# A two-layer decoder on one core: new order of steps in the first layer's woven rounds

## What is computed

```python
x = x + kernel_attention(layernorm(x))        # A
x = x + cross_attention(layernorm(x), ctx)    # B, one head
h = layernorm(x, scale, shift)
x = x + causal_attention_16_heads(h)          # C, on the layernormed value of x
x = ... + moe(layernorm(.., scale, shift))    # D: router, 8 experts, top 2
```

## Time and profile before

| | us |
|---|---|
| median of 3 runs | 1689.74 (1689.53 to 1692.46) |
| profiled execution | 1689.45, its span 1687.8 |
| PE busy | 1285.4 (76%) |
| DVE busy | 998.3 (59%) |
| ACT busy | 522.3 (31%) |
| POOL busy | 415.1 (25%) |
| mean granted clock of PE | 0.857 |

### The profile page before, as it was taken

One profiled execution on the slowest core, in us unless ns is written; L12 is line 12 of the kernel. 1 busy time (PEld: TensorE's weight loads), 2 busy tenths in 40 slices (PEclk: granted clock), 3 DMA queues, 4 the chain that ended last, 5 costly groups with the idle time before them and its releaser, 6 DMA issues.

```text
span 1687.8 us, 24678 instructions
## 1 busy us (share of the span) xinstructions
PE 1285.4 (76%) x7936; PEld 890.2 (53%) x7936; DVE 998.3 (59%) x2156; ACT 522.3 (31%) x1279; POOL 415.1 (25%) x528
## 2 busy tenths in 40 slices
PE   2677868767877699981458977779787697986987
PEld 1554654644644366651237754467554475644755
DVE  4447557457455233325676765768656686677852
ACT  2214324324322222210125512346213363233620
POOL 1032143243253200006622111311212212032100
PEclk9778878878888799995679989779897799987988
DMA  9510010191014211101315310044100350104501
GB/s 376 217 28 1 19 28 13 34 408 49 25 46 198 59 47 44 44 29 45 117 39 98 86 40 12 10 101 111 40 12 2 86 122 21 32 11 88 114 5 46
DMA packets 69693, 122.37 MB, mean 73 GB/s; under 512 B 25404, under 2 KB 55100, under 8 KB 68032
## 3 DMA queue, kind: packets, MB, share of 16 engines
q1 hardware_dynamic: 63936, 110.04, 21.7%
q0 software_dynamic: 5632, 10.77, 2.3%
HBM read 67.69 MB, written 53.07 MB: 72 GB/s over the span
## 4 chain that ended last, share of the span: by engine, by line
PE 46%; issue 24%; DVE 12%; POOL 8%; DVEq 3%; ACT 3%; DMA 2%; POOLq 2%; SPq 0%; ACTq 0%
PE ps L1143 7%; PE ps L1390 5%; PE ps L1162 3%; PE ps L525 3%; PE ps L1316 3%; PE ps L1332 3%; PE ps L533 2%; POOL experts L1779 2%; PE ps L1302 2%; PE ps L1403 2%; PE ps L933 1%; PE ps L1041 1%; POOL headbd L681 1%; PE ps L504 1%; DVE probs L1999 1%
## 5 line engine op out<-in xcount | busy, mean ns | idle before, releaser
L1628 ACT ACTIVATE probs<-ps,small 100x361 f32<-100x361 f32 x256 | 141.3, 557 | 94.1 <-DVE small L2347 89.5
L2347 DVE TENSOR_REDUCE small<-ps 100x2 f32<-100x722 f32 x128 | 115.7, 906 | 36.2 <-PE ps L1302 36.2
L1143 PE MATMUL ps<-every,xT_t 128*128 x256 | 122.3, 601 | 0.4 <-issue 0.4
L1390 PE MATMUL ps<-hT,experts 128*128 128x400 f32 x288 | 117.1, 558 | 1.2 <-DVE small L730 1.2
L1316 PE MATMUL ps<-cst,probs 100*121 100x100 f32 x768 | 104.0, 271 | 8.1 <-DVE probsT L2355 7.7
L1316 PEld LDWEIGHTS ps<-cst,probs 100*121 100x121 f32 x768 | 94.8, 185 | 22.2 <-issue 13.7
L2355 DVE TENSOR_SCALAR probsT<-ps 121x600 f32<-121x600 f32 x128 | 99.2, 775 | 9.1 <-PE ps L1316 9.1
L1332 PE MATMUL ps<-probsT,values_ 121*32 121x100 f32 x1536 | 90.8, 253 | 0.9 <-DVE probsT L2355 0.9
L1302 PE MATMUL ps<-k_stack,q_stack 96*100 96x362 f32 x256 | 81.8, 400 | 6.3 <-ACT probs L1628 5.6
L473 POOL TENSOR_TENSOR small<-small,cst 100x2 f32<-100x2 f32 x56 | 11.1, 198 | 295.3 <-DVE small L453 295.2
L1390 PEld LDWEIGHTS ps<-hT,experts 128*128 128x128 f32 x288 | 59.6, 215 | 42.2 <-issue 14.1
(11 more groups left out here) (329 smaller groups left out, 2887.2 us busy)
## 6 DMA issues: line engine op xcount, KB each, us to landing
k_stack<-key_d SPq DMA_DIRECT2D x192, 90.5 KB, 3.1
tok_d<-wt SPq DMA_DIRECT2D x1, 14848.0 KB, 45.5
res_d<-wt SPq DMA_DIRECT2D x1, 14848.0 KB, 42.0
every<-e_d SPq DMA_DIRECT2D x8, 1536.0 KB, 11.6
ctxT<-ctxT_d SPq DMA_DIRECT2D x8, 726.0 KB, 4.3
key_d<-k_hi SPq DMA_DIRECT2D x32, 181.0 KB, 2.8
key_d<-k_lo SPq DMA_DIRECT2D x32, 181.0 KB, 3.4
gates<-gate_d SPq DMA_DIRECT2D x28, 200.0 KB, 4.4
```

Of the source, the lines that this page charges most:

```text
L1143: ins = e.matmul(ps[:, 2 * i + t % 2, :], xT_t[:, t % 2, c, :], every[:, bass.ds(base + (i * DC + c) * HID0, HID0)], start=(c == 0), stop= ...
L1390: ins = e.matmul(bank(2 * i + j % 2, n=NT), w[:, c, :], hT[:, c, :], start=(c == 0), stop=(c == DC - 1))
L1628: ins = e.activation(f_e[:, n % 2, i, 0:LC], bank(2 * (n % 2) + i, S, LC), ACT.Exp, bias=h_nm[:, n % 2, i:i + 1], accum_out=h_sum[:, b, h: ...
L2347: inc(e.tensor_reduce(h_nm[:, n % 2, 0:2], ps[0:S, 2 * (n % 2):2 * (n % 2) + 2, 0:LC], AX, ALU.max, negate=True), "F_nm")
```

## The change

- Each round takes its steps in the order behind, early half 0, behind, early half 1. 20 rounds instead of 18; all three passes are written out, no hardware loop.
- A's norm for the next group is done ahead, in early's steps 14 (statistics) and 16 (applied) on DVE, its root on POOL in 14; `norm_ahead` for group 0 stands before everything. `xin` is waited for there. A's turn on PE is now step 0, input product 1, and so on.
- The router later: its first half in behind's step 4, its second in attention step 0 (9), PE's products in that step behind the scores; PE waits for `r_placed` in attention step 3, POOL in step 7, and sends in steps 7, 9, 11 and 13 to 17. The reciprocal sums are spread on POOL in attention steps 12 and 18.
- Empty steps: in early at 4, 11 and 16 (on PE), in behind one or two ahead of the attention, and behind C's output and D's scores. Attention is 9 to 27 of 40.
- One sine for both halves (64x400), in early's step 4 of half 0, waiting for both angles.
- The quotients late: the exponentials of A and B are turned and multiplied undivided; each output is scaled by the reciprocal of its sum while it is added (two fused operations of 100x256 for each half). `A_p` and `B_p` go; `B_x` is new: PE waits for it before A's input product writes the same PSUM banks.

Order of PE's steps, before: round 13 `kq0 rT0 kq1 rT1`, 14 `Bs0 Co0 Bs1 Co1`, 15 `pT0 - pT1 -`, 16 `oT0 Dt0 oT1 Dt1`, 17 `out0 gate0 out1 gate1`. After: round 14 `rT0 kq0 rT1 kq1`, 15 `- Bs0 Co0 Bs1`, 16 `Co1 - - -`, 17 `- pT0 Dt0 pT1`, 18 `Dt1 oT0 gate0 oT1`, 19 `gate1 out0 - out1` (kq keys times query, rT the turned reciprocals, Bs scores of B, Co output product of C, pT and oT B's turn and context product, Dt D's turn, 0 and 1 the halves).

The diff, without the places where only empty steps are added:

```diff
@@ -98,7 +98,8 @@
...
 EXPERT_AT = (E1 - 1, *range(E1 - 1))
-ROUNDS, STEPS = 18, 19
+ROUNDS, STEPS = 20, 19
+SEND_AT = {7: 0, 9: 1, 11: 2, 13: 3, 14: 4, 15: 5, 16: 6, 17: 7}
@@ -147,7 +148,7 @@
...
     for _ in range(ROUNDS):
-        for st in (x0, y, x1, y):
+        for st in (y, x0, y, x1):
@@ -401,11 +402,11 @@
...
             names["A_" + n] = names.pop("A_" + sem_name)
-        for n in ("nm", "e", "p", "pTp", "pT", "oTp", "oT"):
+        for n in ("nm", "e", "pTp", "pT", "oTp", "oT"):
...
                 names[f"{stage_}_{n}"] = names.pop(f"{stage_}_AB{n}")
-        for n in ("kqTp", "kqT", "qbkp", "qbk", "s"):
+        for n in ("kqTp", "kqT", "qbkp", "qbk", "s", "x"):
@@ -923,10 +924,11 @@
...
                 p, q, t, bs = 2 * h, 2 * h + 1, tok(h), list(enumerate(seqs(h)))
-                yield
...
                 W(e, "A_hT", g, 1, h)
+                if g:
+                    W(e, "B_x", g - 1, 1, h)
@@ -959,7 +962,7 @@
...
                 yield
-                W(e, "A_p", g, 1, h)
+                W(e, "A_e", g, 1, h)
@@ -998,7 +1002,8 @@
...
                 yield
-                W(e, "B_p", g, 1, h)
+                yield
+                W(e, "B_e", g, 1, h)
@@ -1031,7 +1036,7 @@
...
-            def attend(g):
+            def attend(g, routed):
@@ -1071,24 +1076,24 @@
...
                         scores(n)
+                    if routed and n == 0:
+                        ahead(g - 1)
...
                         turn(n - 2)
+                    if routed and n == 3:
+                        e.wait_ge(r_placed.sem, r_placed.at(g - 1))
...
             def behind(g, routed):
-                yield
-                if routed:
-                    ahead(g - 1)
-                yield
+                for _ in range(3):
+                    yield
...
                     W(e, "C_hT", g, 1, h)
-                    if h == 1 and routed:
-                        e.wait_ge(r_placed.sem, r_placed.at(g - 1))
@@ -1096,10 +1101,12 @@
...
                 yield
-                yield from attend(g)
+                yield
+                yield from attend(g, routed)
...
                     yield
+                yield
@@ -1112,11 +1119,11 @@
...
                     yield
+                yield
...
             in_turn(early(0, 0), early(0, 1))
-            woven(early(1, 0), early(1, 1), behind(0, False))
-            with e.Fori(1, NG - 1) as g:
-                woven(early(g + 1, 0), early(g + 1, 1), behind(g, True))
+            for g in range(NG - 1):
+                woven(early(g + 1, 0), early(g + 1, 1), behind(g, g > 0))
@@ -1436,8 +1442,10 @@
...
                 yield
-                W(e, "A_ang", g, 1, h)
-                inc(e.activation(a_trig[:, t], a_ang[:, t], ACT.Sin), "A_trig")
+                yield
+                if h == 0:
+                    W(e, "A_ang", g, 1, 1)
+                    e.activation(a_trig, a_ang, ACT.Sin).then_inc(names["A_trig"].sem, 2)
@@ -1514,21 +1524,21 @@
...
                 yield
+                yield
...
                     yield
-                for _ in range(4):
+                for _ in range(5):
...
                     yield
-                yield
-                yield
+                for _ in range(3):
+                    yield
...
             in_turn(early(0, 0), early(0, 1))
-            woven(early(1, 0), early(1, 1), behind(0))
-            with e.Fori(1, NG - 1) as g:
+            for g in range(NG - 1):
@@ -1680,23 +1690,23 @@
...
             def early(g, h):
-                root_pool(e, "A_", g, h)
-                yield
-                if h == 0:
-                    e.wait_ge(ld["rows"].sem, 16)
-                W(e, "A_xn", g, 1, h)
-                inc(add_bias(x, xin, "A_out", h), "A_xb")
...
                 inc(e.tensor_tensor(a_rn[:, own(h)], a_ss[:, own(h)], cs("mhalf", S)[:, 0:HB], ALU.pow), "A_rn")
-                yield
-                for _ in range(7):
+                e.wait_ge(ld["rows"].sem, 16)
+                inc(add_bias(x, xin, "A_out", h), "A_xb")
+                yield
+                for _ in range(8):
...
                 yield
+                for _ in range(2):
+                    yield
+                if g + 1 < NG:
+                    root_pool(e, "A_", g + 1, h)
@@ -1720,16 +1730,21 @@
...
                 strips(0)
-                if routed:
-                    e.wait_ge(r_placed.sem, r_placed.at(g - 1))
+                yield
...
                         strips({1: 1, 7: 2, 11: 3}[n])
-                    if routed and n % 2 and n >= 3:
-                        send((n - 3) // 2)
+                    if n == 12:
+                        recips_pool(e, "C_", g, 0, 1)
+                    if n == 18:
+                        recips_pool(e, "C_", g, 1, 2)
+                    if routed and n == 7:
+                        e.wait_ge(r_placed.sem, r_placed.at(g - 1))
+                    if routed and n in SEND_AT:
+                        send(SEND_AT[n])
@@ -1740,25 +1755,23 @@
...
                     yield
-                yield
-                yield
+                for _ in range(3):
+                    yield
                 yield from attend(g, routed)
-                for h in range(2):
-                    recips_pool(e, "C_", g, h, h + 1)
-                    yield
-                yield
-                yield
+                for _ in range(4):
+                    yield
...
                     yield
-                for _ in range(4):
-                    yield
-
+                for _ in range(6):
+                    yield
+
+            for h in range(2):
+                root_pool(e, "A_", 0, h)
...
             e.wait_ge(ld["fill"].sem, 16)
-            woven(early(1, 0), early(1, 1), behind(0, False))
-            with e.Fori(1, NG - 1) as g:
-                woven(early(g + 1, 0), early(g + 1, 1), behind(g, True))
+            for g in range(NG - 1):
+                woven(early(g + 1, 0), early(g + 1, 1), behind(g, g > 0))
@@ -1885,12 +1898,15 @@
...
+            def norm_ahead(g, h):
+                e.wait_ge(ld["x"].sem, g * 16 + 16)
+                inc((yield from norm_dve(e, "A_", g, h, xin, xnX)), "A_xn")
+                yield
+
...
                 p, q, t, o = 2 * h, 2 * h + 1, tok(h), own(h)
-
-                if h == 0:
-                    e.wait_ge(ld["x"].sem, g * 16 + 16)
-                inc((yield from norm_dve(e, "A_", g, h, xin, xnX)), "A_xn")
+                norm = norm_ahead(g + 1, h) if g + 1 < NG else iter(())
+
@@ -1950,20 +1967,23 @@
...
                 yield
-                W(e, "A_e", g, 1, h)
-                e.reciprocal(a_rs[:, o], a_sum[:, o])
-                e.drain()
-                inc(e.tensor_tensor(lg, lg, a_rs[:, o].unsqueeze(2).broadcast_to([S, HB, S]), ALU.mult), "A_p")
...
                 W(e, "A_xb", g, 1, h)
-                add_out(x, p, h)
+                e.reciprocal(a_rs[:, o], a_sum[:, o])
+                e.drain()
+                for i, b in enumerate(seqs(h)):
+                    e.scalar_tensor_tensor(x[:, b, :], ps[0:S, p, i * D:(i + 1) * D], a_rs[:, b:b + 1], x[:, b, :],
+                                           ALU.mult, ALU.add)
+                e.drain()
                 inc((yield from norm_dve(e, "B_", g, h, x, xnX)), "B_xn")
+                yield
...
                 inc(e.tensor_scalar(b_qbk[:, o], bank(p, S, HB), 1.0, None, ALU.mult), "B_qbk")
+                next(norm, None)
@@ -1973,21 +1993,23 @@
...
                 yield
-                W(e, "B_e", g, 1, h)
-                e.reciprocal(b_rs[:, o], b_sum[:, o])
-                e.drain()
-                for b in seqs(h):
-                    ins = e.tensor_scalar(b_e[:, b, 0:LC], b_e[:, b, 0:LC], b_rs[:, b:b + 1], None, ALU.mult)
-                inc(ins, "B_p")
+                next(norm, None)
+                yield
...
                 W(e, "B_xb", g, 1, h)
-                e.tensor_tensor(xall[:, bass.ds(g * NB + HB * h, HB), :], tokens(q), x[:, o, :], ALU.add)
-                e.drain()
-                yield
-
-            def attend(g):
+                e.reciprocal(b_rs[:, o], b_sum[:, o])
+                e.drain()
+                for i, b in enumerate(seqs(h)):
+                    ins = e.scalar_tensor_tensor(xall[:, bass.ds(g * NB + b, 1), :].rearrange("p o n -> p (o n)"),
+                                                 ps[0:S, q, i * D:(i + 1) * D], b_rs[:, b:b + 1], x[:, b, :],
+                                                 ALU.mult, ALU.add)
+                inc(ins, "B_x")
+                e.drain()
+                yield
+
+            def attend(g, ways):
@@ -2014,32 +2036,33 @@
...
                         inc(e.reciprocal(h_rs[:, o, :], h_sum[:, o, :]), "C_rs")
+                    if n == 0:
+                        next(ways, None)
...
                 norms = [norm_dve(e, "C_", g, h, group, y) for h in range(2)]
-                next(norms[0])
-                next(ways, None)
-                yield
```

(20 more changed lines are left out.)

4 lines of the change are left out of this document (added).

## The result

The changed kernel takes 1680.7 us (median; 1680.4 to 1685.9) against 1689.7 for the kernel before: ratio 0.9947, 95% interval 0.9926 to 0.9967. A second comparison on another chip gave 0.9940 (0.9923 to 0.9957). So it is 9 to 10 us faster where 36 were forecast, and lies outside the range. The profiled execution after took 1685.9 (span 1684.2).

The account below looks back on a forecast made before the run. No engine is full: a pass is a chain of hand-overs between four in-order engines, mostly PE waiting for DVE. Passes -38.7, start +0.8, last group +1.8 give -36.1 us: 1653.4 us, range 1634 to 1674.

Parts of the forecast that it names:

- the three kinds of waits: PE's waits for A's divided probabilities and the quotient product gone, those for normed rows at B's turn near 0.
- mark to step 0: Pass start, norm ahead and router later: step 0 at 28.1 us instead of 33.2, -5.1; without router 25.2 instead of 31.1.
- Clock: PE's new idle stretches put ten microseconds of following work partly at half rate: +2.5 us a pass, bounds 0 and +6.
- Slower: Rival: DVE-paced rounds leave PE at the low level from step 5 to 18, +13 us a pass, 1728 us; 4%.
- Late quotients: In A, division leaves DVE's path between exponential and turn; PE's 10.7 us wait over six halves goes: -3.6 us a pass.
- the quotient product: B's late quotients and rear step first make it ready when PE asks; 12.0 us of waits go: -4.0 us a pass.
- The empty step: Behind A's output, one more round lets two attention steps in before B's turn, removing PE's waits: -3.6 us a pass.
- One sine: Steps 0 to 4: two table loads a pass fewer, both angles made before step 0; 15.8 us for four steps, -1.9.
- Start and last group: Kernel start +0.8 us (first combine product waits for the second sine), last group +1.8 us (router's second half in bare steps).
- Half of it: Rival: DVE takes the place, PE's removed waits return as waits for score evaluation; -19 us in all, 1670 us; 20%.
- sign of failure, a pass above 118 us: The prediction called itself wrong if a woven pass took above 118 us; it expected passes of 108 to 113.

Follow-up runs that it names:

- the filling: Changed kernel with 24 extra 100x400 bf16 matmuls on PE ahead of D's first turn in each of the four groups: ratio 0.9849, 1663 to 1671 us.
- the later norm: Changed kernel with the last half of the next group's first norm one round later on VectorE: ratio 0.9906.
- the front-first trace: Changed kernel with the order inside a round put back to front half 0, rear, front half 1, rear: ratio 0.9897, with all ten runs 0.9944.
- the late quotients alone: Kernel before with only the division of A's and B's weights dropped and each output scaled in its addition: ratio 0.9894.
- the masks moved: Changed kernel with GpSimd's second and later key masks and two value strips held back until the next group's second angle is done: ratio 0.9951.
- the waits for the sine were filled: Changed kernel with extra matmuls ahead of D's first turn, C's first turn, the shell rows' turn and comb: ratio 0.9829.

## Why the prediction was wrong

The direction held, and of the single signs most: the three kinds of waits went, step 0 comes 28.6 us behind the mark (forecast 28.1; -4.3 for -5.1), D's turn waits 4.97 us (forecast 4), two table loads a pass. The misses by stretch, from PE's timelines, in us for the three passes (before to after):

| stretch | measured | forecast |
|---|---|---|
| mark to step 0 | -7.0, -4.3, -5.1 | -5.9, -5.1, -5.1 |
| step 0 to 4 | +0.3, +1.4, +0.3 | -1.9 each |
| step 4 to kq | -2.8, -3.9, -5.8 | -7.2 each |
| kq to the mark | +5.2, +5.1, +3.0 | +2.3 each |

(The forecasts of 13.9 and 12.9 for the outer passes hold another 1.2 and 1.0 that its terms don't itemize.) Mis-sized were these terms:

*Clock, +2.5 a pass with a bound of +6.* This is the step that failed. In the tail of a pass alone it costs 5.8, shown by the filling: 17.4 us, 10 more than the sum held, though just inside the bound. The spells ahead of kq come on top: up to 3 us in a pass, 4.7 in all, by comparison with the trace that has none (the later norm). That makes some 22 us where the sum held 7.5, the largest part of the 25 missed in the passes. I took "ten microseconds of following work partly at half rate"; it is all the work to the mark, 15 us of it, and wholly. The row that I rested on, 3.17 us behind a wait of 1.99, is of a spell that ended within the next line: that takes 1.93 us for its twelve matmuls, where such a line takes 1.42 at the high level and 2.84 (six in 1.42) at the low one. The granted clock is 0.60 over the product and 0.94 from 329.27 to the mark:
```profile
329.27 1.93 PE L1004 MATMUL ps<-cst,values_ 100*121 100x100 f32 x12
```
I carried over what that short spell cost. The Trainium skill (TensorE: Matmul & The Clock Gate, HAM oscillation) says that a gap puts the array back to half rate and the next burst starts cold; at D's turn the trace agrees. I gave this only the rival of 4%, as if it struck throughout or not at all.

*Late quotients, -3.6 a pass for A.* Too small inside the change. I counted the waits' length (10.7 us). Alone, steps 8 to 12 gave 2.9 us; in the new order putting the division back costs 3.0, 4.8 and 5.9 us there, as a low spell begins behind it, and 7 to 9 us a pass with B's. That is 25 us in all, and the kernel with everything but the quotients is at 1.0090: all the rest of the change together costs 15 us, where the forecast had it at -25 (-36.1 + 3 x 3.6). The 4.0 a pass of the quotient product stay in that rest: those waits are 1.3 us there too, and 2.3 us in the front-first trace, against 12.0 with the late quotients alone. So neither B's late quotients nor the rear step first removed them, as the forecast had it, but the other new steps; which of them was not taken apart.

*The empty step, -3.6, with A's quotients -3.6.* Step 4 to kq went from 48.3 to 45.3, 44.4 and 42.2 us (forecast 41). In the three passes of the trace without a low spell on steps 4 to 8 it is 42.2 to 42.8, so the step is short by one to two microseconds at the high level, and by up to four with a spell.

*One sine, -1.9.* Steps 0 to 4 took 18.0 where 15.8 were forecast. Two things were missed: VectorE's angle lines are held by GpSimd's masks, which now run just then (3.2 us; before, one line of 1.55 us), and the table load no longer runs ahead of the wait (1.3 us). But the experiments took both away and gained nothing in the passes. I had priced this stretch by VectorE's chain; behind it steps 4 to 8 took the gain back, at clocks of 0.50 to 0.76 with the masks moved. That the clock alone takes it was not tested there.

*Start and last group, +2.6 together.* They are +3.6 and +4.4. Of the start only that the sine now stands behind both angles and its own load was read (it began at 42.53, behind the angle's end at 42.45; before, the load was over when the angle came); its first mark scatters by 3 us. In the last group PE waits 6.88 us for C's first rows and then 2.03 us behind the router's second half, and runs its steps 2 and 3 at the low level; this was not taken apart.

The sum for the middle pass: 28.6 + 18.0 + 44.4 + 30.9 = 121.8. The last stretch before was 25.7, the forecast 28.0, with the fill 25.0.

*Rivals.* "Half of it" named VectorE as what takes the place; where the waits for the sine were filled this is what seems to have happened, at the tail it is not. "Slower" had the right mechanism, but placed it in steps 5 to 18, where the clock was 0.90 and 0.94. The forecast's own sign of failure, a pass above 118 us, came true in all three.
